# Graph attention layer: edge scores with features along partitions, and a walk in pieces of 256 edges

## What is computed

```python
h = maximum(layernorm(x), 0)
xm = h @ W_n2m.T;  ea = rbf @ W_r2m.T
loop_attr = segment_sum(ea, dst) / maximum(deg, 1)      # each node gets a loop edge
xl = xm @ Wl.T + bl;  xr = xm @ Wr.T + br;  e = ea_f @ We.T
u = leaky_relu(xl[src_f] + xr[dst_f] + e, 0.2)          # per edge, 8 heads x 16
logits = einsum('ehd,hd->eh', u, att)
p = exp(logits - segment_max(logits, dst_f)[dst_f])
alpha = p / segment_sum(p, dst_f)[dst_f]
out = segment_sum(xl[src_f] * alpha, dst_f) + bias
return x + out @ W_m2n.T
```

## Time and profile before

| | us |
|---|---|
| median of 3 runs | 2800.05 |
| profiled execution | 2797.73 |
| its span, first to last instruction | 2795.8 |
| PE busy | 1988.0 (71%) |
| DVE busy | 2120.6 (76%) |
| POOL busy | 1971.4 (71%) |
| ACT busy | 1334.6 (48%) |
| granted PE clock, mean of the span | 0.83 |

### The profile page before, as it was taken

One profiled execution on the slowest core, in us unless ns is written; L12 is line 12 of the kernel. 1 busy time (PEld: TensorE's weight loads), 2 busy tenths in 40 slices (PEclk: granted clock), 3 DMA queues, 4 the chain that ended last, 5 costly groups with the idle time before them and its releaser, 6 DMA issues. The chain is left out here.

```text
span 2795.8 us, 67636 instructions
## 1 busy us (share of the span) xinstructions
PE 1988.0 (71%) x16862; PEld 1711.1 (61%) x16863; DVE 2120.6 (76%) x5075; ACT 1334.6 (48%) x4076; POOL 1971.4 (71%) x1886
## 2 busy tenths in 40 slices
PE   1947777777777777677777777777767677776776
PEld 0636666666666666666666666666666566666654
DVE  6957777787787877877778777787777877777666
ACT  0645554544545545454554545545455454454212
POOL 0357777777777777777777777777777777777313
PEclk9966888888888888888888888888888988888757
DMA  4233333333333333333333333323333333333135
GB/s 152 84 74 67 71 71 67 75 68 72 70 67 75 67 71 72 68 75 67 71 71 67 76 68 71 71 66 74 67 72 71 69 75 66 71 70 68 30 113 168
DMA packets 302694, 210.41 MB, mean 75 GB/s; under 512 B 165834, under 2 KB 268172, under 8 KB 302254
## 3 DMA queue, kind: packets, MB, share of 16 engines
q0 software_dynamic: 57728, 125.73, 20.0%
q1 hardware_dynamic: 241251, 76.69, 11.8%
q10 hardware_dynamic: 3275, 3.01, 0.3%
HBM read 190.76 MB, written 16.12 MB: 74 GB/s over the span
## 5 line engine op out<-in xcount | busy, mean ns | idle before, releaser
L663 POOL DMA_INDIRECT xl_g<-xl_table,meta x1804 | 1909.0, 1058 | 563.0 <-issue 548.9
L744 PE MATMUL banks<-msg,onehot 128*128 128x177 f32 x3608 | 823.8, 382 | 13.3 <-DVE msg L840 13.3
L744 PEld LDWEIGHTS banks<-msg,onehot 128*128 128x128 f32 x3608 | 703.4, 236 | 26.3 <-DVE msg L840 18.0
L690 PE MATMUL banks<-Wc,rbfT 32*128 32x136 f32 x3608 | 264.6, 364 | 633.2 <-DVE z L819 498.7
L690 PEld LDWEIGHTS banks<-Wc,rbfT 32*128 32x128 f32 x3608 | 172.5, 210 | 712.0 <-issue 448.2
L757 ACT ACTIVATE distance<-iota_n,minus_slot 128x128 f32<-128x128 f32 x1804 | 573.1, 396 | 44.5 <-DVE minus_slot L814 22.9
L767 ACT ACTIVATE msg<-rbf 128x128 f32<-128x128 f32 x451 | 139.8, 310 | 747.8 <-PE banks L744 743.6
L693 PE MATMUL banks<-xr_parts,onehotT 128*128 x5412 | 480.7, 249 | 0.0
L693 PEld LDWEIGHTS banks<-xr_parts,onehotT 128*128 128x128 bf16 x5412 | 386.7, 110 | 71.7 <-issue 26.9
L819 DVE TENSOR_TENSOR z<-banks,xl_g 128x544 f32<-128x544 f32 x451 | 323.9, 718 | 126.2 <-DMA xl_g<-xl_table,meta 123.0
L848 DVE TENSOR_REDUCE u_sum<-u_att 128x32 f32<-128x512 f32 x451 | 309.5, 686 | 15.6
(11 more groups left out here) (183 smaller groups left out, 1988.2 us busy)
## 6 DMA issues: line engine op xcount, KB each, us to landing
rbf<-in_edge_attr SPq DMA_DIRECT2D x451, 64.0 KB
xl_g<-xl_table,meta POOLq DMA_INDIRECT x1804
masks<-masks_dram SPq DMA_DIRECT2D x451, 24.1 KB
meta<-meta_dram SPq DMA_DIRECT2D x451, 4.0 KB
x_sb<-in_x SPq DMA_DIRECT2D x6, 1024.0 KB, 21.8
x_in<-in_x SPq DMA_DIRECT2D x6, 896.0 KB, 7.4
out<-result SPq DMA_DIRECT2D x6, 896.0 KB, 5.1
xl_table<-lr_sb SPq DMA_DIRECT2D x49, 68.0 KB, 1.6
```

What stands on the lines that cost most here:

```text
L663: pool.indirect_dma_start(out=xl_g[:, s % RING, t], out_offset=None, in_=xl_table, in_offset=bass.IndirectOffsetOnAxis(ap=meta[:, s, 0, t: ...
L690: nc.tensor.matmul(z_ps[:, t], rbfT[q, n], Wc[q], start=True, stop=False)
L744: mm = nc.tensor.matmul(U_ps, onehot[:, j % RING, t], msg[:, j % 2, t], start=t == 0, stop=t == TILES - 1)
```

## The change

- A step is now two pieces of 256 edges (`SPLIT`, `PIECE`), and each piece has a window of its own. There are 806 pieces, 854 entries of the walk, and 427 steps.
- z is computed transposed: features along partitions, 256 edges of a piece along the row. PE sums three things in PSUM: six bf16 matmuls with `xr_parts` held still and 256 columns of `onehotT`, four fp32 matmuls of 64 rows for the attributes, and four fp32 matmuls that add the gathered rows (`xl_g` held still, the identity moving, 128 columns each).
- ACT takes relu and DVE makes u (both per half of 256 columns). PE applies att: one fp32 matmul with 512 columns per step writes the 8 rows of that step and adds zeros to the other rows of the batch, so no transpose of logits is left. The 8 extra columns of `xl_table` go.
- `onehotT` comes from one DVE comparison of a broadcast row of slots (`slot_bc`, a new load of 128 x 512 bf16 per step) with the partition's number. Its transposes on PE and copies on ACT go. `onehot` is made later, just before it is used.
- In one turn of its loop PE now does, in this order: every eighth turn four small matmuls behind a wait for the long scans (`run_done`), and in the turn after that two more behind a wait for the short scans (`ends_listed`); the transpose of the next step's attributes; z of step k; att for step k-1; the sums of step k-15; every eighth turn the eight transposes of the batch's weights.
- The lag between z and the messages is 15 steps instead of 12; the ring of `xl_g` has 24 places instead of 16.
- The weights are read by the messages from PSUM, after exp has been taken before the transpose.
- The source indices and the slots of all steps are laid out in SBUF in the prologue: the walk table comes first, then eight indirect gathers of rows of `meta_dram`, conversions on DVE, transposes on PE, copies on ACT, and small DMAs from SBUF to SBUF that fetch each row's neighbours (`halo_in`). The masks are built from these rows, step by step of the walk. POOL's loop is written out without a register and waits for no load.

The core of the diff (some waits and the parts of the batch that only move by a piece are left out):

```diff
+            for k, s, r in sweep(sp, 0, 4 * BATCH, STEPS, MASK_ROWS, UNROLL, UNROLL):
+                if inside(k, STEPS):
+                    if inside(k - RING, STEPS):
+                        sp.wait_ge(attr_ready, TICK * (k - RING + 1))
+                    for h in range(SPLIT):
+                        e = sp.value_load(edge_tab[0:1, one(SPLIT * k + h)], min_val=0, max_val=E - PIECE)
+                        sp.dma_start(rbf[:, s % RING, h * PT * D_RBF:(h + 1) * PT * D_RBF],
+                                     edge_attr[bass.DynSlice(e, PIECE), :].rearrange("(p i) k -> p (i k)", i=PT)
+                                     ).then_inc(loads[s % RING], 16)
+                    if inside(k - SRING, STEPS):
+                        sp.wait_ge(ohT_ready, k - SRING + 1)
+                    sp.dma_start(slot_bc[:, s % SRING], slot_dram[one(k)].broadcast_to([P, GROUP])
+                                 ).then_inc(slots_in[s % SRING], 16)
...
-            for k, s, r in sweep(pool, 0, UNROLL, STEPS, STEPS, UNROLL, UNROLL):
-                full = settled(pool, (r + 1) * FULL)
...
+            pool.wait_ge(set_up, SET_UP)
+            for k in range(STEPS):
+                if k >= RING:
...
+                    e = TILES * k + t
+                    pool.indirect_dma_start(out=xl_g[:, k % RING, t], out_offset=None, in_=xl_table,
+                                            in_offset=bass.IndirectOffsetOnAxis(ap=src_tab[:, e:e + 1], axis=0)
+                                            ).then_inc(gathers[k % RING], 16)
...
                 if has(b):
+                    par, R = half(s)
+                    found, taken = settled(pe, b + 1), settled(pe, b)
+                    pe.wait_ge(set_up, SET_UP)
+                    pe.wait_ge(run_done, found)
...
+                b = batch_at(s, r, 3)
+                if has(b):
+                    par, R = half(s)
                     pe.wait_ge(ends_listed, b + 1)
...
+                if inside(k + 1, STEPS):
+                    n = (s + 1) % RING
+                    pe.wait_ge(loads[n], (r * (UNROLL // RING) + (s + 1) // RING + 1) * FULL)
+                    if inside(k, STEPS):
+                        pe.wait_ge(rbfT_ready, k + 1)
+                    nc.tensor.transpose(rbfT_ps, rbf[:, n], ident[:]).then_inc(rbfT_done, 1)
...
+                    pe.wait_ge(ohT_ready, k + 1)
+                    if inside(k - 1, STEPS):
+                        pe.wait_ge(u_ready, Z * k)
+                    for h in range(SPLIT):
+                        for part in range(PARTS):
+                            nc.tensor.matmul(z_ps[h], parts_of(xr_parts, w[h], part),
+                                             onehotT[:, n, h * PIECE:(h + 1) * PIECE], start=part == 0, stop=False)
+                    pe.wait_ge(rbfT_ready, k + 1)
+                    for i in range(PT):
+                        for h in range(SPLIT):
+                            q = slice(h * PT * D_RBF, (h + 1) * PT * D_RBF)
+                            nc.tensor.matmul(z_ps[h][:, i::PT], Wc2[q, i], rbfT[q, n], start=False, stop=False)
+                    pe.wait_ge(gathers[s % RING], (r * (UNROLL // RING) + s // RING + 1) * GATHERED)
+                    for h in range(SPLIT):
+                        for i in range(PT):
+                            mm = nc.tensor.matmul(z_ps[h][:, i::PT], xl_g[:, s % RING, h * PT + i], ident[:],
+                                                  start=False, stop=i == PT - 1)
+                        mm.then_inc(z_done, 2 + h)
...
+                    pe.wait_ge(u_ready, Z * k)
...
+                    nc.tensor.matmul(LT_ps[par * ROWS:(par + 1) * ROWS],
+                                     att_pad[:, ROWS - HEADS - i * HEADS:2 * ROWS - HEADS - i * HEADS], uT[:, n],
+                                     start=i == 0, stop=last).then_inc(L_done, 1)
+                if inside(k - LAG, STEPS):
+                    j = s - LAG
+                    pe.wait_ge(msg_ready, TICK * (k - LAG + 1))
+                    pe.wait_ge(attr_ready, TICK * (k - LAG + 1))
+                    pe.wait_ge(oh_ready, TICK * (k - LAG + 1))
+                    if inside(k - LAG - 1, STEPS):
+                        pe.wait_ge(added, TICK * (k - LAG))
+                    for h in range(SPLIT):
+                        for i in range(PT):
+                            t = h * PT + i
+                            mm = nc.tensor.matmul(U_ps[h], onehot[:, j % 2, t], msg[:, j % 2, t],
+                                                  start=i == 0, stop=i == PT - 1)
+                        mm.then_inc(agg_done, 1 + h)
...
+                if inside(k + 1, STEPS):
+                    act.wait_ge(rbfT_done, k + 2)
+                    if inside(k - 1, STEPS):
+                        act.wait_ge(z_done, Z * k)
+                    nc.scalar.activation(rbfT[:, (s + 1) % 2], rbfT_ps, ACT.Copy).then_inc(rbfT_ready, 1)
...
+                    if inside(k - LAG - 1, STEPS):
+                        act.wait_ge(agg_done, TICK * (k - LAG))
+                    if inside(k - LAG, STEPS):
+                        act.wait_ge(oh_ready, TICK * (k - LAG + 1))
+                    for t in range(TILES):
+                        nc.scalar.activation(distance[:, t], iota_n[:], ACT.Abs,
+                                             bias=minus_slot[:, one(TILES * (k - LAG + 1) + t)]).then_inc(dist_ready, 1)
...
+                    act.wait_ge(dist_ready, TILES * (k - LAG + 2))
+                    nc.scalar.activation(onehot[:, m % 2], distance[:], ACT.Relu, scale=-1.0, bias=1.0
+                                         ).then_inc(oh_ready, TICK)
...
+                if inside(k, STEPS):
+                    for h in range(SPLIT):
+                        act.wait_ge(z_done, Z * k + (2, Z)[h])
+                        if inside(k - 1, STEPS):
+                            act.wait_ge(u_ready, Z * (k - 1) + (2, Z)[h])
+                        nc.scalar.activation(relu[:, h], z_ps[h], ACT.Relu, scale=1.0 - SLOPE).then_inc(relu_ready, 2 + h)
...
+                    n, q = (s + 1) % 2, (s + 1) % SRING
+                    dve.wait_ge(slots_in[q], (r * (UNROLL // SRING) + (s + 1) // SRING + 1) * 16)
+                    if inside(k - 1, STEPS):
+                        dve.wait_ge(z_done, Z * k)
...
+                    nc.vector.tensor_scalar(onehotT[:, n], slot_bc[:, q], node_of[:], None, ALU.is_equal
+                                            ).then_inc(ohT_ready, 1)
...
+                    nc.vector.tensor_tensor(to[:, :, :, 0:D_HEAD],
+                                            xl_g[:, m % RING].rearrange("p t (h d) -> p t h d", d=D_HEAD),
+                                            w_ps[:, :, row].unsqueeze(3).broadcast_to([P, TILES, HEADS, D_HEAD]),
+                                            ALU.mult).then_inc(msg_ready, TICK - 1)
+                    nc.vector.tensor_copy(to[:, :, :, D_HEAD:HC], wm_ps[:, :, row]).then_inc(msg_ready, 1)
...
+                        dve.wait_ge(agg_done, TICK * a + (1, TICK)[h])
+                        if inside(a - 1, STEPS) or h:
+                            dve.wait_ge(added, TICK * a + h)
+                        nc.vector.tensor_tensor(at(acc, w_sum[h]), at(acc, w_sum[h]), U_ps[h], ALU.add
+                                                ).then_inc(added, 1 + h)
...
-                    dve.wait_ge(z_done, k + 1)
-                    dve.wait_ge(gathers[s % RING], (r * (UNROLL // RING) + s // RING + 1) * GATHERED)
-                    nc.vector.tensor_tensor(z[:, s % 2], z_ps, xl_g[:, s % RING], ALU.add).then_inc(z_ready, 1)
...
+                    for h in range(SPLIT):
+                        dve.wait_ge(relu_ready, Z * k + (2, Z)[h])
+                        if h == 0 and inside(k - 2, STEPS):
+                            dve.wait_ge(L_done, k - 1)
+                        nc.vector.scalar_tensor_tensor(out=uT[:, s % 2, h * PIECE:(h + 1) * PIECE], in0=z_ps[h],
+                                                       scalar=SLOPE, in1=relu[:, h], op0=ALU.mult, op1=ALU.add
+                                                       ).then_inc(u_ready, 2 + h)
...
+                    dve.wait_ge(L_done, min(b * BATCH + BATCH, STEPS) if isinstance(b, int) else b * BATCH + BATCH)
+                    dve.wait_ge(masks_in[par], pairs * BATCH * 16)
+                    nc.vector.tensor_tensor_scan(forth[R], masks[R, 0:GROUP], LT_ps[R], -BIG, ALU.add, ALU.max
...
+                    nc.vector.tensor_tensor_scan(run_max[R, ::-1], masks[R, GROUP:0:-1], forth[R, ::-1], -BIG,
+                                                 ALU.add, ALU.max).then_inc(run_done, 1)
```

And in the prologue:

```diff
+            sp.wait_ge(halo_set, 2)
+            sp.wait_ge(keys_ready, CHUNKS * SPLIT)
+            r, c = chunk_rows[-1], CHUNKS - 1
+            for to, of, there, here in ((0, GROUP, 0, 1), (GROUP + 1, 1, 1, 0)):
+                for n, chunks in ((P, slice(0, c)), (r, slice(c, CHUNKS))):
```

(18 more changed lines are left out.)

817 lines of the change are left out of this document (396 added, 421 removed).

## The result

The changed kernel takes 2982.8 us (median of four executions, 2982.1 to 2990.4), the kernel before beside it 2797.3. The ratio is 1.068, 95% interval 1.064 to 1.071: slower, against a forecast of 0.945, and outside the forecast's range of 2515 to 2860 us. In a later pair the two took 2983.9 and 2788.5 us, 1.071 (1.067 to 1.074). The profiled execution has a span of 2988.6 us. Many of the later kernels ran on occasions on which every kernel, that of before too (3594 to 3683 us), stood idle more between its instructions while the operations themselves were no longer, so of these only the ratio to the kernel before beside them is used (the changed kernel itself was never run on one of them).

A forecast was written before the change was run, and what follows sets the result against it. POOL bounds the old kernel, PE the changed one at 5.33 us a step: 190 us to the first gather, 2276 walk, 55 drain, 119.3 finale, 1.9 beyond the span; forecast 2643 us, range 2515 to 2860.

The forecast's parts named there:

- The bound before, and POOL: Walk: POOL bounds the old kernel at 5.45 us a step; with fewer slowed gathers it needs 5.1.
- Rivals 1 and 2: POOL stays the bound: gathers keep their price, 2693 us, chance 0.22; or PE hardly stalls, POOL at floor, 2523, 0.12.
- What would show it: Walk signs: POOL waits for msg, gathers below 1.0 us, PE busy over 85%, clock above 0.9, first gather about 190.
- Prologue and finale: Before and after the walk: prologue 161.7 us plus 28, so first gather at 190; finale unchanged at 119.3.
- Rival 4: Prologue: the long row of single-element DMAs delays the start, +60 us instead of +28, total 2675; chance 0.07.
- plain turns: PE's turns in the walk without stalls: transpose, xr, attributes, gathered rows, att and sums, together 4.54 us a step.
- waits for DVE's scans: PE stalls per batch: 1.7 us behind the long scans, about 0.9 behind the short ones, together 2.6.
- half clock: PE in the walk: one clock dip a batch after a stall, worth 1.3 to 3 us, taken as 1.8.
- The bound of 5.0: PE's computing work per step in the walk: upper bound 5.0 us, lower 4.3, around the estimate of 4.54.
- the waits at the head of PE's turn: PE's waits for DVE's scans, everything on PE queued behind them, z of the next step too: 2.6 us a batch.
- Rival 3: Walk: batch stalls hold PE's clock at 0.84, 6.0 us a step, 2928 us, slower than before; chance 0.14.
- Drain: After the walk: 16 steps without z at half clock, sums 2.6 us, adding 0.33, two hand-overs, 3.3 each; 55 taken.

The follow-up runs named there:

- the combination: Changed kernel with PE's small matmuls behind z, loop written out for 192 steps, DVE's register loads at its turn's head: 2631.9 us, 0.943 of before.

## Why the prediction was wrong

**The bound before, and POOL.** Right. POOL's price fell to 0.967 + 0.305 a gather, 5.09 us a step (5.1 forecast), its waits for msg came, and the steps fell to 427. Rivals 1 and 2 both supposed that POOL stays the bound; it does not. Nearly all that was named under "What would show it" as a sign of being right came: waits for msg, gathers below 1.0 us, PE busy 91% of the walk, a clock of 0.95, the first gather at 183.5 us. None of these signs looks at what PE's queue does besides computing.

**Prologue and finale.** 183.5 for 190 us, 118.9 for 119.3. Rival 4 did not happen.

**PE's turn.** The sum of a batch, forecast and measured:

| us per eight turns | forecast | measured |
|---|---|---|
| plain turns | 36.3 | 39.2 |
| the batch's own matmuls | 2.0 | 2.1 |
| waits for DVE's scans | 2.6 | 1.6 |
| register loads behind an empty queue | - | 2.8 |
| half clock | 1.8 | 1.6 |
| rest | - | 0.5 |
| sum | 42.7 | 47.8 |

5.1 us a batch, 53 batches, are 270 us; seven jumps at 10.0 are 70. Together 340, against 331 of the stages.

1. *The plain turn was costed too low*, 4.54 for 4.90, 154 us over the walk. Three terms share most of it: the gathered rows 1.09 (0.97), att 1.00 (0.90), the attributes 0.65 (0.55). The first two were carried down, and across, on a slope of 1.7 ns a column fitted to 136 and 177 columns. 512 columns cost 1.00, so the plain ratio (0.95) was nearer there; 128 columns cost 0.27 each, more than the slope or the ratio gives (0.24) and more than the 0.26 of 136 columns. Why is not shown. The sums, whose row was at hand, were exact. The bound of 5.0 held.
2. *The step that failed in its mechanism* is the one that took the waits at the head of PE's turn, with the clock, for the whole price of a stall. The plain turn was only mis-sized; here a cost was left out. The waits' mechanism was right, and they were even shorter than forecast (1.6 for 2.6). But the change also puts two register loads between the transpose and xr. In plain turns they are hidden, as PE's queue runs ahead of its array; after each wait they stand bare. The prediction listed the instructions that PE computes with and not those that its queue alone executes. By the table the bare loads are 148 us; moving them is worth 194, with the clock that comes back. The kernel before had one such load in PE's turn (L683); there POOL was the bound and hid what PE lost.
3. *The clock.* One dip a batch and its size were right (1.6 for 1.8), but its cause was put down to the waits for DVE. It needed the bare loads too: without them L836 stays at 1.16 us. Rival 3 names a time near the result, 2928, for a reason that did not happen: the clock in the walk rose from 0.84 to 0.95.
4. *The jumps* are missing altogether: 70 us. In the kernel before every gap of POOL is 0.3 us, so whatever PE or DVE lost at a jump did not hold POOL up. When a bound moves to another engine, everything that this engine did beside the old bound comes into the sum. The Trainium skill ("Runtime: NRT & Kernel Launch", Instruction fetch mechanics) says that a taken branch whose target isn't at hand waits for it to be fetched; the 3.55 to 4.97 us of idle at the jumps agree, though no run shows that it is the fetching, and it gives no price.

**Drain.** 79 us for 55. The forecast had 3.3 us a turn; this is one:

```profile
2829.28 2.70 PE L858 MATMUL banks<-msg,onehot 128*128 128x177 f32 x8 [2.02 <-DVE acc L991]
...
2832.09 0.69 DVE L974 TENSOR_TENSOR msg<-xl_g,banks 128x512 f32<-128x512 f32 x1 [1.62 <-PE banks L858]
...
2833.58 0.34 DVE L991 TENSOR_TENSOR acc<-acc,banks 128x177 f32 x1 [0.66 <-issue]
```

The half-clock sums were right (2.70). Left out were the message and the second add between one turn's sums and the next's, and DVE's bare loads (0.66); a turn is 5.34 us.

**What would have been right.** With the stalls, the loads and the jumps gone, PE's own work alone remains: 39.2 + 2.1 a batch and small gaps, 42.1 measured, 5.29 us a turn, and 2632 us. POOL is just behind it, at 5.09 us a turn. That this is near the forecast of 2643 is luck, two errors against each other: work 0.36 us a turn too small, and stalls counted that the combination does not have.

## What to carry to other kernels

List for the engine that will be the bound everything its queue executes, register loads and jumps too, and ask at each wait what stands between it and the next large operation: what is hidden in a full queue is bare behind a wait. Put register loads ahead of waits, and a wait for another engine behind the longest work that does not need it; here the first was worth 194 us and the second 294, without removing any work. When the bound moves to an engine, its idle time in the old profile has to be costed afresh.

## What the hardware did that was not expected

- Two register loads on PE cost 1.2 us behind a wait (1.16 and 1.17), nothing in a plain turn; on DVE one pair takes 0.66 us in the drain.
- Each register load takes 0.30 us on PE's sequencer, and a pair with its register work 1.4 us.
- A jump back over a body of 48 or 192 turns holds PE for up to 5.0 us, and DVE at the same time for 3.95; the turns around it lose 8 to 11 us together, half-clock work included.
- A gather is held up by a product or a copy of SBUF tiles if it is running when the gather begins (up to 1.46 and 1.20 us instead of 0.94), and not by a later one; a copy late in a gather is itself held up (0.66 us instead of 0.42).
- On some occasions every kernel took 29 to 37% longer with the same length of each operation: a matmul of L858 on average 335 and 332 ns in the same kernel on the same chip at 3681 and 2689 us. What differed is idle time on PE, DVE and ACT; its cause was not found.
